# A wavelet, convolution and median kernel: a plane of x in rounded parts, batch norm 3 three steps earlier, and five additions done by transfers into DRAM

## The reference

```
cA, cH, cV, cD = dwt2(x)                       # Haar transform, 4 bands of 16x16
proc = lambda c: batchnorm_relu(einsum('bchw,oc->bohw', c, conv_w), bn_gamma, bn_beta)
rimg0 = idwt2(proc(cA), proc(cH), proc(cV), proc(cD))
rimg1 = x taken apart by three Haar levels and put together again   # which gives x
y = conv3x3(concatenate([rimg0, rimg1], axis=1), convW_w) + convW_b # 256 -> 128 channels
x = batchnorm_relu(y, bnW_gamma, bnW_beta)
d = median_blur(x, 3)                          # of 9 neighbours, zeros outside
return x + einsum('bchw,oc->bohw', d, W) + b
```

## Time and profile before

| what | value |
|---|---|
| median of 3 runs | 400.87 us (400.85 to 400.98) |
| profiled execution, its own time | 403.58 us |
| profiled execution, its span | 401.2 us |
| PE busy | 383.8 us, 96% |
| DVE busy | 372.2 us, 93% |
| POOL busy | 232.5 us, 58% |
| ACT busy | 170.8 us, 43% |
| written to DRAM | 8.39 MB, all of it after 361 us |

### The profile page before, as it was taken

How to read it: one execution, slowest core, us unless ns; L and a number is a source line. 1 busy time by engine, 2 the same in 40 slices (tenths; PEclk the granted TensorE clock), 3 DMA queues, 4 the chain that set the end, 5 groups by cost and what they waited for, 6 DMA issues and landing times.

```text
span 401.2 us, 3603 instructions
## 1 busy us (share of the span) xinstructions
PE 383.8 (96%) x1106; PEld 205.1 (51%) x1106; DVE 372.2 (93%) x487; ACT 170.8 (43%) x351; POOL 232.5 (58%) x213
## 2 busy tenths in 40 slices
PE   6889999999999999999999999999999999998776
PEld 2245578866454555555555545454545464443222
DVE  2889967999999999999999999999999999999994
ACT  2456674446252433333334343333424221379661
POOL 3999559460694664738474747465564740016791
PEclk9999999999999999999999999999999999999988
DMA  7980010010101001010101010101011000002665
GB/s 290 418 364 2 2 52 2 0 52 2 53 1 52 17 37 52 0 52 0 54 0 52 1 54 1 52 1 52 8 46 33 19 2 1 0 0 119 247 248 223
DMA packets 7793, 26.69 MB, mean 67 GB/s; under 512 B 992, under 2 KB 1248, under 8 KB 7776
## 3 DMA queue, kind: packets, MB, share of 16 engines
q1 hardware_dynamic: 7776, 26.48, 17.6%
HBM read 18.09 MB, written 8.39 MB: 66 GB/s over the span
## 4 chain that ended last, share of the span: by engine, by line
PE 81%; DVE 12%; POOL 3%; DMA 2%; issue 1%; SPq 0%; ACT 0%; DVEq 0%
PE conv_ps L429 60%; PE conv_ps L444 12%; PE one_ps L411 4%; PE one_ps L530 3%; DVE y L1004 2%; PE conv_ps L554 2%; DMA z<-x 2%; POOL y L241 1%; POOL y L242 1%; DVE one_ps L916 1%; DVE one_ps L925 1%; DVE sorted_cols L876 1%; DVE sorted_cols L923 1%; DVE one_ps L910 1%; DVE sorted_cols L883 1%
## 5 line engine op out<-in xcount | busy, mean ns | idle before, releaser
L429 PE MATMUL conv_ps<-ru,wt 128*128 128x512 f32 (+1 forms) x324 | 129.9, 537 | 0.0
L429 PEld LDWEIGHTS conv_ps<-ru,wt 128*128 128x128 f32 x324 | 61.3, 190 | 55.1 <-issue 52.7
L429 PE MATMUL conv_ps<-xu,wt 128*128 128x496 f32 (+3 forms) x216 | 86.6, 537 | 0.0
L663 ACT ACTIVATE y<-conv_ps,sgn 128x512 f32<-128x512 f32 (+1 forms) x36 | 24.4, 679 | 124.1 <-PE conv_ps L429 124.1
L429 PEld LDWEIGHTS conv_ps<-xu,wt 128*128 128x128 f32 x216 | 41.0, 190 | 35.6 <-issue 33.7
L248 POOL TENSOR_TENSOR ru<-z 128x512 f32<-128x512 f32 x14 | 18.2, 1301 | 59.3 <-DVE one_ps L916 59.3
L342 POOL TENSOR_TENSOR ru<-eo 128x512 f32<-128x512 f32 x16 | 17.0, 1062 | 47.5 <-DVE one_ps L874 47.4
L429 PE MATMUL conv_ps<-ru,v 128*128 128x496 f32 (+3 forms) x108 | 43.3, 537 | 0.0
L554 PE MATMUL conv_ps<-z,w 128*128 128x512 f32 x64 | 32.7, 653 | 7.4 <-POOL z L387 4.1
L411 PE MATMUL one_ps<-y,w 128*128 128x512 f32 x64 | 30.5, 601 | 5.1 <-POOL y L242 1.8
L620 ACT ACTIVATE z<-z,bn 128x256 f32<-128x256 f32 x64 | 33.1, 595 | 0.4 <-DVE bn L819 0.4
(11 more groups left out here) (141 smaller groups left out, 741.1 us busy)
## 6 DMA issues: line engine op xcount, KB each, us to landing
z<-x SPq DMA_DIRECT2D x16, 512.0 KB, 10.5
raw_place<-x SPq DMA_DIRECT2D x15, 512.0 KB, 3.2
out<-y SPq DMA_DIRECT2D x15, 512.0 KB, 2.6
wt<-w_t SPq DMA_DIRECT2D x2, 576.0 KB, 10.8
ru<-x SPq DMA_DIRECT2D x1, 512.0 KB, 14.1
out<-y SPq DMA_DIRECT2D x2, 256.0 KB, 2.6
w<-w_t SPq DMA_DIRECT2D x2, 64.0 KB, 7.9
vec<-vectors SPq DMA_DIRECT2D x1, 3.0 KB, 8.3
```

The costliest lines, as they stand in the source:

```text
L429: return nc.tensor.matmul(bank(u, b)[:, (r0 - row) * BW:(r1 - row) * BW], taps(half, kx, ky), plane[:, (r0 + dy) * BW:(r1 + dy) * BW], sta ...
L663: S.activation(at(slot(n), row * W + b, [[2, cols]]), src, ACT.Identity, scale=sgn[:, :], accum_out=y_sum[:, part:part + 1]).then_inc(y_ke ...
```

## The change

Four things are changed together.

1. `outputs` does the products of u0 of x in rounded parts for the images 4 to 14 (`SPLIT0`). ACT rounds the plane into the first half of `x_hi` (`u0_hi`), POOL makes the remainder in the first half of `x_lo` (`u0_lo`), the taps are rounded once into `w0_hi` and `w0_lo`. As the buffers are shared with `round_x` and `make_lo`, `round_x(n + 2)` now comes after bank 0 of image n. `u0_lo` waits for DVE's new semaphore `highs_read` (L908 has been done).
2. The second copy of an image of x is loaded into `zslot(n)`, which is free by then, instead of `raw_place`, which is gone.
3. `BN3_AT` is 8 instead of 11 and `FINISH_AT` is shifted too. L908 isn't counted as a step any more. The mix of image 15 goes to a bank of its own (`one_ps`).
4. `SUMMED` is (1, 3, 5, 7, 10) instead of (1, 3, 7, 9, 12). For these SP sends the mapped y alone, and when it has landed, POOL's queue starts a transfer that adds the mix to it in DRAM. POOL's five additions L393 and L398 are gone.

```
+    SPLIT0 = tuple(range(4, IMAGES - 1))
-    SUMMED = (1, 3, 7, 9, 12)
+    SUMMED = (1, 3, 5, 7, 10)
-    BN3_AT, FINISH_AT = 11, (15, 17, 19, 21, 23, 25, 27, 29)
+    BN3_AT, FINISH_AT = 8, (12, 14, 16, 18, 21, 23, 26, 28)
...
+        u0_hi, u0_lo = x_hi[:, 0:HALF], x_lo[:, 0:HALF]
+        w0_hi, w0_lo = (sb(n, [CH, KY * CH], fp32r) for n in ("w0_hi", "w0_lo"))
...
-            return ru03[1] if n == 1 else raw_place
+            return ru03[n][:, :] if n < 2 else zslot(n)
...
+            ahead = list(SUMMED)
+            for n in OWN[:-1]:
+                while ahead and ahead[0] < n + 3:
+                    m = ahead.pop(0)
+                    sp.wait_ge(x1_by_act, SUMMED.index(m) + 1)
+                    sp.dma_start(out_img[:, m, :], slot(m)).then_inc(x1_sent[m], 16)
+                sp.wait_ge(out_ready, OWN.index(n) + 1)
...
+            def make_u0_lo(n):
+                pool.wait_ge(highs_read, last_unit(n - 1) + 1)
+                pool.wait_ge(u0_hi_made, SPLIT0.index(n) + 1)
+                G.tensor_tensor(u0_lo, xu03[n % 2][:, 0:HALF], fl(u0_hi), ALU.subtract).then_inc(u0_lo_made, 1)
...
+            def add_mix(n):
+                pool.wait_ge(mix_kept, SUMMED.index(n) + 1)
+                pool.wait_ge(x1_sent[n], 16)
+                G.dma_start(out_img[:, n, :], zslot(n), accum_op=ALU.add).then_inc(mix_sent[n], 16)
...
-                    G.tensor_tensor(slot(n - 3), slot(n - 3), zslot(n - 3), ALU.add).then_inc(out_by_pool, 1)
+                    add_mix(n - 3)
...
+            def u0_products(u, part, parts_taps):
+                n, row, rows = UNITS[u]
+                for ky in KY_ORDER:
+                    dy = ky - 1
+                    r0, r1 = max(row, -dy), min(row + rows, H - dy)
+                    mm = nc.tensor.matmul(bank(u, 0)[:, (r0 - row) * BW:(r1 - row) * BW], parts_taps[:, ky * CH:(ky + 1) * CH],
+                                          part[:, (r0 + dy) * BW:(r1 + dy) * BW], start=False, stop=False, skip_group_check=True)
+                return mm
...
+                    if rounded:
+                        pe.wait_ge(u0_hi_made, SPLIT0.index(n) + 1)
+                        u0_products(u, u0_hi, w0_hi)
+                        u0_products(u, u0_hi, w0_lo)
...
+                    if rounded:
+                        pe.wait_ge(u0_lo_made, SPLIT0.index(n) + 1)
+                        mm = u0_products(u, u0_lo, w0_hi)
                     mm.then_inc(y_done, 1)
...
                 for b in range(2):
                     keep_y(u, b)
+                    if b == 0 and n + 2 in SPLIT and n in SPLIT0:
+                        round_x(n + 2)
...
                 if u == last_unit(n):
+                    if n + 1 in SPLIT0:
+                        act.wait_ge(p_done, last_unit(n + 2) + 1)
+                        S.activation(u0_hi, xu03[(n + 1) % 2][:, 0:HALF], ACT.Identity).then_inc(u0_hi_made, 1)
...
-                step(V.tensor_tensor(p2, pair(col_hi, 0), pair(col_hi, 1), ALU.min))
-                after(1)
+                V.tensor_tensor(p2, pair(col_hi, 0), pair(col_hi, 1), ALU.min).then_inc(highs_read, 1)
+                after()
```

More of the change, by code:

```diff
@@ L195, in wavelet_conv_median_kernel @@
         mix_kept = sem("mix_kept")
-        out_by_pool = sem("out_by_pool")
+        x1_sent, mix_sent = ({n: sem(f"{name}{n}") for n in SUMMED} for name in ("x1_sent", "mix_sent"))
         out_ready = sem("out_ready")
@@ L214, in raw, with outer_left_taps, w0_part @@
         def raw(n):
-            return ru03[1] if n == 1 else raw_place
+            return ru03[n][:, :] if n < 2 else zslot(n)
+        def outer_left_taps():
+            return at(wt[:, :], X_HALF * KY * KX * CH, [[KX * CH, KY], [1, CH]])
+        def w0_part(t):
+            return at(t[:, :], 0, [[CH, KY], [1, CH]])
         def fl(t):
@@ L283, in _ @@
                 sp.dma_start(out_img[:, IMAGES - 1, half], slot(IMAGES - 1)[:, half]).then_inc(out_sent, 16)
-            sp.wait_ge(out_sent, 16 * (IMAGES + 1))
+            sp.wait_ge(out_sent, 16 * (len(OWN) + 1))
+            for n in SUMMED:
+                sp.wait_ge(mix_sent[n], 16)
         @block.gpsimd
@@ L337, in make_ru03 @@
                 G.tensor_tensor(odd, u1, u2, ALU.subtract).then_inc(eo_made, 1)
+            def make_ru03(n):
+                k = n % 2
                 pool.wait_ge(eo_made, n + 1)
@@ L502, in outputs @@
                 for b in range(2):
-                    for ky in KY_ORDER:
-                        product(u, b, X_HALF, (0, 2)[b], planes(xu03[n % 2][:, :])[b], ky, onto=True)
+                    rounded = b == 0 and n in SPLIT0
+                    if rounded:
+                        if n == SPLIT0[0]:
+                            pe.wait_ge(w0_lo_made, 1)
+                        pe.wait_ge(u0_hi_made, SPLIT0.index(n) + 1)
+                        u0_products(u, u0_hi, w0_hi)
+                        u0_products(u, u0_hi, w0_lo)
+                    else:
+                        for ky in KY_ORDER:
+                            product(u, b, X_HALF, (0, 2)[b], planes(xu03[n % 2][:, :])[b], ky, onto=True)
                     if b == 0:
@@ L545, in _, with mixed, mix @@
             outputs(len(UNITS) - 1)
-            def mix(n, k):
+            def mixed(n):
+                return one_ps[:, 0, :] if n == IMAGES - 1 else conv_ps[:, n % 2, :]
+            def mix(n):
                 if 0 < n < IMAGES - 1:
@@ L553, in mix @@
                     half = slice(b * BANK, (b + 1) * BANK)
-                    mm = nc.tensor.matmul(conv_ps[:, k, half], w2[:, :], zslot(n)[:, half], start=True, stop=True)
+                    mm = nc.tensor.matmul(mixed(n)[:, half], w2[:, :], zslot(n)[:, half], start=True, stop=True)
                     if b == 1 or n == IMAGES - 1:
@@ L564, in _ @@
             for n in range(2):
-                mix(n, n)
-            for n in range(2, IMAGES):
+                mix(n)
+            for n in range(2, IMAGES - 1):
                 if n - 2 in SUMMED:
@@ L570, in _ @@
                     pe.wait_ge(out_ready, OWN.index(n - 2) + 1)
-                mix(n, n % 2)
+                mix(n)
+            mix(IMAGES - 1)
         @block.scalar
@@ L646, in _ @@
                 S.activation(tap_part(taps_hi, b), whole_taps(b), ACT.Identity).then_inc(hi_taps_made, 1)
+            S.activation(w0_part(w0_hi), outer_left_taps(), ACT.Identity).then_inc(w0_hi_made, 1)
             act.wait_ge(bn1_ready, 1)
@@ L1003, in finish @@
                 v = slot(n)[:, first:first + count]
-                V.scalar_tensor_tensor(v, v, cb2, conv_ps[:, n % 2, first:first + count], ALU.max, ALU.add).then_inc(out_ready, 1)
+                V.scalar_tensor_tensor(v, v, cb2, (one_ps[:, 0, :] if n == IMAGES - 1 else conv_ps[:, n % 2, :])[:, first:first + count], ALU.max, ALU.add).then_inc(out_ready, 1)
             place = {BN3_AT: second_batch_norm}
```

54 lines of the change are left out of this document (29 added, 25 removed).

## The result

| | median | runs |
|---|---|---|
| before, same chip | 400.93 us | 400.76 to 401.93 |
| changed kernel | 398.25 us | 396.31 to 399.0 |
| ratio | 0.9914 | 95% interval 0.9889 to 0.9939 |

The change makes the kernel 2.6 us faster. The forecast was 393.0 us (390 to 398): the sign is right, the gain was to be 7.9 us. The six runs of the changed kernel lie 2.7 us apart, the six of before beside them 1.2.

The account below looks back on a forecast made before the run. The prediction took PE alone as the second stage's bound, DVE close behind, and DVE as the third stage's chain. It summed -6.3 (steps 2 to 4 of the path, BN3 and medians) and -1.6 (end) to -7.9: 393.0 us, range 390 to 398.

Parts of the forecast that it names:

- Step 1: Second stage, `outputs`: u0 in rounded parts saves PE 5.2 us over 11 images, with no wait of PE.
- Rival C: PE gains nothing in `outputs`, by waiting for `u0_lo` or slower groups; 398 us, chance 0.09.
- Step 2: Second stage: POOL's `eo` delays DVE's median, but the loss regulates itself; DVE stays 1.3 us late and PE the bound.
- Rival B: The meeting of POOL and DVE doesn't regulate itself, so BN3 comes 5 us later; 398 us, chance 0.10.
- Step 3: BN3 begins at 347.3 instead of 353.19 us, -5.9 us, with three instructions (2.34 us) moved behind it.
- Waits of PE in `outputs`: Sign in the second stage: the prediction is wrong if PE shows waits in `outputs`; no size given.
- Step 4: Third stage, medians behind BN3: removing POOL's additions frees DVE's L908 and L916, 2.7 us gained (bounds 0 and 3.5).
- Step 5: The end, last median instruction to last finish: 4.8 instead of 6.4 us, with image 15's mix in its own bank, -1.6 us.
- Rival A: The end keeps the full clock and crowded finishes cost nothing; 390.7 us, chance 0.12.
- Step 6: Third stage: an adding transfer takes 2.6 us of all DMA engines (1.3 to 3.9), its issue on POOL 1 us.
- rival D: Slow adding transfers let the DMA engines end the kernel; at 6 us each 407.3 us, chance 0.09.

Follow-up runs that it names:

- e1: The kernel before, unchanged, profiled a second time; 400.95 us.
- e10: The changed kernel, unchanged, measured and profiled once more; 398.57 us.
- e2: The changed kernel with u0 in plain fp32 again (SPLIT0 empty); 401.9 us.
- e4: The changed kernel with the banks of image 15 seeded at the earlier place in the median of image 13; 397.85 us.
- e5: The changed kernel with ACT making `x_hi` ahead of `keep_y` of bank 0 instead of behind it; 396.99 us.
- e7: The changed kernel with POOL's five adding transfers left out, so five mixes are missing from the output; 395.53 us.
- e8: The changed kernel with each of POOL's adding transfers issued one image later; 396.95 us.
- e3: The changed kernel with the five mixes added by POOL again instead of by adding transfers, same images; 398.25 us.
- e11: The changed kernel with POOL's five adding transfers made plain ones, so five outputs are the mixes alone; 396.7 us.
- e9: The changed kernel with the edits of e4, e5 and e8 together; 395.77 us.

## Why the prediction missed

Against e1 and the first profile of the changed kernel, the miss divides into three terms. Measured: BN3 317.08 - 321.40 = -4.3 us from PE's first product, and 0.45 us less before it, which the change didn't make (31.22 against 31.67 us; in e10 it was 31.75); the stretch 40.89 - 38.60 = +2.3, the end 3.9 - 4.1 = -0.2: together -2.7, and the medians say -2.6. Forecast: -5.9, 2.34 - 2.7 = -0.4, and -1.6: -7.9. So BN3, the stretch and the end are off by 1.6, 2.7 and 1.4 us, less those 0.45 of luck: 5.2.

*Step 1, u0 on PE: right but for image 4, 0.4 us.* The round of ACT's `keep_y` of bank 0 from image 4 on is 18.74 us where it was 19.22, as forecast. Image 4 itself gains nothing: its round is 19.16 us. `u0_lo` comes too late for it, because DVE is 3.9 us late at image 3, and not at most 3 as the step reckoned. The 0.9 us more come from what the step cost at nothing, the rounding of `w0`: it pushes POOL's `eo` onto DVE's L990 in the first median, which takes 1.46 us where L916 took 0.39 in e1, in the timelines of POOL and DVE (read from the rows; no run leaves the rounding out, and in e2, which has it too, DVE is as late):

```profile
65.58 1.15 POOL L391 TENSOR_TENSOR w_lo<-wt,w_hi 128x384 fp32r<-128x384 f32 x1
```

```profile
70.97 1.46 DVE L990 TENSOR_TENSOR one_ps<-sorted_cols 128x224 f32<-128x224 f32 x1
```

e2 puts the worth of the step, with what it does to DVE, at 3.7 us in BN3's begin and in the time. Rival C is out.

*Step 2, DVE's lateness: right in mechanism and size.* The meeting settles at a loss of some 0.3 us an image, though not in every image, only from about image 9 on, and DVE is 1.1 us late there (forecast 1.3). The median of image 14 began at 337.32 us (forecast 337.7). Rival B is out. By the rule of the Trainium skill, "SBUF — State Buffer", "Who interferes with whom", L947 would be held for as long as `eo` still runs: 280.30 + 1.28 - 281.10 = 0.48 us by the rows, and it was longer by 0.33; the trace agrees roughly.

*Step 3, BN3: 1.2 us off.* The step looked only at what DVE must have ready for BN3, and not at what a late DVE owes PE. L921 seeds the bank of image 15, and the `outputs` of 15 follow those of 14 with no `pq` in between, so that this seed alone has no slack. A DVE that is 1.1 us late makes PE wait 0.95 us there, and `keep_y` of image 15 follows that of image 14 after 11.3 us where it was 10.1 in before and is in e4: 1.2 us. e4 and e5 remove it by two ways, and BN3 gains 1.2 us by either. With the 0.4 us of image 4 this is the 1.6. Waits of PE in `outputs` were one of the prediction's own signs of being wrong; both are such waits.

*Step 4, the medians behind BN3: the step that failed most, +2.7 us.* The 2.7 us of POOL's additions were a real gain (e7). They were given back, since the adding transfer brings a wait of its own on POOL: for the landing of x1. I had named this wait's neighbours (the corners, `map_x1`) and priced only the issue, at 1 us (measured 0.87 to 1.01). The wait itself has no row in before, and wasn't bounded. It is 1.5 to 3.5 us at the fourth transfer, bunches two or three maps, and DVE's instruction with two inputs in SBUF stands behind all of them. That the wait is the cause is shown for 1.5 of the 2.6 us that the transfers cost (e8); the rest are the meetings that e8 still has, L988 1.54 and L990 1.01 us. The range for this step (0 to 3.5 gained) held the result, 40.94 - 40.89 = 0.05 gained; the value in it was chosen from the wrong side.

*Step 5, the end: +1.4 us.* 6.4 us at the low clock was a feature of the one profiled execution, which most runs of the kernel don't share. The prediction took a gain from that execution and subtracted it from a median that never contained the loss. The sign stood in the numbers: its own time was 403.58 us, 2.7 above the median, while I compared the span with the median and called the difference 0.3. In the runs of the changed kernel the time is the span plus 2.0 us. Rival A said that the end would keep the full clock, and expected a gain from it; it is true, and gains nothing against the median. (The terms of the step at full clock add up to 3.8 us, not 3.9; measured 3.9. Those of rival A give 390.5 us, not 390.7.)

*Step 6, the adding transfers: between the bounds.* 3.0 us where I took 2.6. Nothing waits for them at the end, so rival D is out; what they do is to fill the queue. The busy time by stretch shows it:

```profile
360.00:370.00 10.00, 8.61 (x20) 3.44 (x19) 9.93 (x11) 10.00 (x11) 5.61 (x10) 1.00 0.88 249
370.00:380.00 10.00, 6.08 (x13) 2.18 (x12) 10.00 (x9) 8.94 (x9) 7.33 (x13) 0.96 1.06 303
```

The share of the 16 DMA engines (the last number but one) is 0.88 and then 1.06. I had compared the sum of the transfers with the whole time in which data is there (34 of 37 us) and looked at the end alone; in the middle the plain stores then landed late, 4.6 us after their issue (median) against 2.7 in e3 and in e11. The Trainium skill, "Collectives: The Full Stack", "The bandwidth ceiling: the fold count and why AG ≠ RS ≠ AR", would give half the rate of a copy, 2 x 1.29 = 2.6 us; it was measured in a different setting, and here the factor is 3.0 / 1.29 = 2.3.

What stays open: why e4's median is only 0.4 us lower where its BN3 begins 1.2 us earlier (the first stage's 0.75 us and the pattern of e10 are both larger than the difference), and what makes DVE stand through two maps in the changed kernel and not in e11. That the meetings that are left (about 1.1 us between e9 and e7's stretch) can be placed away from all maps wasn't shown; the one try moved them.

## What to carry to other kernels

Before a gain is subtracted from a median, compare the profiled execution's own time (not its span) with that median, and look at the clock where they differ: a loss that only this execution had can't be won. And before two profiled executions are compared at one instant, count from an event that the change can't touch: here the first stage alone moved by 0.75 us. When work moves from an engine to a transfer, the wait for the data that the transfer needs is the price, not the issue; look at what stands behind it on the issuing engine, and give the wait one more round of slack. And when an engine becomes late by a constant amount, go through everything that it hands out, above all the last one of a loop, where the work that gave slack is missing.
